# The second attention of a four-stage block: exponentials in f16 halves, turned by DMAs, on another timetable

## The chip, the cores and the metric

The kernel runs on one core of a Trainium2 chip. The metric is the device time of one launch in microseconds (us), the median of the timed runs. Engines are TensorE (PE, whose weight loads are PEld), VectorE (DVE), ScalarE (ACT), GpSimd (POOL) and SyncE (SP), which here issues DMAs.

## The reference

The input has 4096 tokens (2 sequences of 2048) of width 512, and for each sequence a context of 154 keys. Four stages add to `x` one after another: a masked attention, a mixture of 64 experts, a second attention without a mask, and a fused expert branch. The change is in the third:

```
x = x + tanh(g_xattn[1]) * attention(layernorm(x), ctx, ctx, wq, wk, wv)
Q = split(q @ wq.T);  K = split(k @ wk.T);  V = split(v @ wv.T)      # 16 heads of 32
attn = softmax(einsum('bhqd,bhkd->bhqk', Q, K) / sqrt(32))           # 2048 x 154 for each head
out = einsum('bhqk,bhkd->bhqd', attn, V)
```

Products that need f32 accuracy are either done in f32, or in f16 as three products of halves (`TERMS`: high by high, high by low, low by high), where a value is held as an f16 number and an f16 rest.

## The kernel before

`second_attention` (L913) works on 8 blocks of 512 tokens. A block has 4 tiles of 128 tokens and 16 heads in two groups of 8, so 8 *units* of one tile by 8 heads, and 64 units in the stage. Per unit:

- TensorE computes the 8 score matrices, 128 x 154 (L1064). They lie in two PSUM halves of 4 heads.
- VectorE takes the maxima of the first half out of PSUM (L1193), copies the second half to `sc` (L1195) and takes its maxima there (L1198).
- ScalarE computes exp(score - maximum) in f32 with the row sums (L1127), writing into `prob`, in which the 8 heads are interleaved. VectorE inverts the sums (L1181).
- The exponentials are needed with the keys on the partitions. TensorE turns them in ten 128 x 128 f32 transposes (L1013, `keys_turned`): one for the first 128 keys of each of 8 heads, and two for the 26 remaining keys of 4 heads together. ScalarE copies one of the three PSUM banks to `pT` (L1137), VectorE the other two (L1210).

Per block, TensorE further projects the queries (L55 with `wq`, 48 f16 matmuls), multiplies the turned exponentials by the values in f32, four groups of 4 heads (L1038 for the first 128 keys, L1040 for the rest, `V` and `VR`), and turns the result back (L1047). ScalarE copies the group's result (L1109), VectorE scales (L1171), GpSimd adds it to `x` (L1222). The rows of the coming blocks are normalised meanwhile: statistics (L126, L132), the normalised row (L148, VectorE), its f16 high half (L157, ScalarE), its low half (L166, VectorE here), and four DMA transposes (L175, SyncE). SyncE also loads a block (L62) and stores one (L1254), 1 MiB each.

Order: `plan` is one list of pieces per step of one unit, shared by all engines (`TURNS`, `VALS`, `FIN`); each engine walks through it in order. `NP = 3` buffers of exponentials, `NS = 2` of score halves. The stage ends with an all-engine barrier. Ahead of it TensorE already does two products of the next stage (`maps_ahead.tensor_first`), whose maps are loaded by `sync_ahead` after the store of block 6.

`first_attention` (L364) does nearly the same work in another form, and its rows are used below: exponentials in f32 (L650), rounded to f16 high halves by ScalarE in even units (L660, L661) and VectorE in odd ones (L774, L775), low halves by GpSimd (L807, L808), one DMA transpose for each half of a unit (L883), values in f16 with three terms (L568, L571), `NP = 2` buffers of halves and a timetable (`WHEN`) with a due time for each piece and engine. It has a mask, biases and an output projection besides.

## Time and profile before

| | |
|---|---|
| timed runs, median (lowest to highest) | 2776.18 us (2774.99 to 2778.49), 3 runs |
| profiled execution | 2766.97 us |
| its span, first to last instruction | 2765.2 us |
| TensorE busy | 2583.6 us (93%) |
| VectorE busy | 1599.7 us (58%) |
| ScalarE busy | 1390.0 us (50%) |
| GpSimd busy | 1121.0 us (41%) |
| mean granted TensorE clock | 0.983 of full speed |
| second attention, from its first maxima to the end of the stage | 1608.7 to 1944.7 us |

The shares over the whole span hide the stages: what bounds the second attention is read from stretches inside it. Busy time is the union of the instructions of an engine; in tables of groups, the means of neighbouring instructions overlap by some tens of ns.

### The profile page before, as it was taken

To read this page: it belongs to the slowest core of one execution; us is meant where nothing else is said; L and a number is where in the kernel's file an instruction comes from. 1 tells how busy PE (TensorE), PEld (TensorE's weight loads), DVE (VectorE), ACT (ScalarE), POOL (GpSimd) and SP (SyncE) were. 2 spreads that over 40 slices of the span, in tenths; PEclk is the share of its full clock that TensorE was granted. 3 is DMA by queue.
4 is the path that set the end of the run, shared out by engine and by line. 5 is a ranking of instruction groups with operands and counts; after the bars stand their busy time and mean duration, and the time that the engine had idled before them with its cause. 6 is when DMAs were issued, how large, how long until landed. Compare 5 with 4: busy or idle time off the path is not lost. (4 is left out here: it accounts for less than half of the span.)

```text
span 2765.2 us, 44090 instructions
## 1 busy us (share of the span) xinstructions
PE 2583.6 (93%) x16830; PEld 1404.4 (51%) x16830; DVE 1599.7 (58%) x2553; ACT 1390.0 (50%) x3074; POOL 1121.0 (41%) x887
## 2 busy tenths in 40 slices
PE   5788878999999999999999979998999999999999
PEld 3333333444444477777777645565444444444444
DVE  6799995655555365656556478887643332334232
ACT  4678884322322166666666468998433222222221
POOL 3577781565555656666666401011102211121111
PEclk8899999999999999999999989999999999999999
DMA  7799987222221299999999731322310111011000
GB/s 190 145 178 203 181 170 219 70 69 63 62 62 47 94 325 284 288 288 283 279 288 273 178 96 58 92 62 86 125 39 16 46 46 35 12 46 46 23 8 31
DMA packets 455409, 353.08 MB, mean 128 GB/s; under 512 B 323104, under 2 KB 332064, under 8 KB 455200
## 3 DMA queue, kind: packets, MB, share of 16 engines
q1 hardware_dynamic: 418336, 282.92, 36.6%
q0 software_dynamic: 36864, 67.34, 11.6%
q8 instruction: 135, 2.21, 0.3%
q14 instruction: 74, 0.61, 0.1%
HBM read 198.86 MB, written 75.89 MB: 99 GB/s over the span
## 5 line engine op out<-in xcount | busy, mean ns | idle before, releaser
L1673 POOL DMA_INDIRECT ids<-sh_tk,sh_su x256 | 267.8, 1046 | 231.0 <-PE sh_gu L55 75.0
L55 PE MATMUL ex_gu<-ex_xT,ex_h 128*128 128x256 f16 x3072 | 345.8, 273 | 2.3 <-ACT ex_xT L1946 1.7
L55 PEld LDWEIGHTS ex_gu<-ex_xT,ex_h 128*128 128x128 f16 x3072 | 300.1, 98 | 51.3 <-ACT ex_xT L1946 2.0
L2620 POOL TENSOR_TENSOR fe_prodT<-fe_pp,fe_prodT 128x512 f16<-128x512 f32 x64 | 77.4, 1210 | 591.3 <-ACT fe_prodT L2405 591.3
L2072 POOL DMA_INDIRECT xp<-ex_oo,ex_to x128 | 236.2, 1845 | 182.6 <-ACT ex_oo L1980 138.7
L1807 DVE SCALAR_TENSOR_TENSOR ex_h<-ring,ex_h 128x1024 f16<-128x1024 f32 x128 | 151.1, 1222 | 155.2 <-ACT ex_h L1797 155.2
L55 PE MATMUL at_g<-hm_zT,hm_w 128*128 128x512 f16 x768 | 184.7, 395 | 23.7 <-issue 16.1
L2536 DVE SCALAR_TENSOR_TENSOR ring<-fe_g,fe_nf,ring 128x512 f32<-128x512 f32 x32 | 24.0, 751 | 293.1 <-PE fe_g L2321 293.1
L55 PE MATMUL ex_o<-ex_h,ex_aT 128*128 128x512 f16 x768 | 181.2, 387 | 0.0
L1781 POOL DMA_INDIRECT ex_xg<-zrows,ex_idxu x128 | 158.3, 1237 | 49.2 <-issue 33.2
L650 ACT ACTIVATE at_s<-at_s,at_mx 128x154 f32<-128x154 f32 x512 | 168.5, 410 | 16.7 <-DVE at_mx L764 16.7
L55 PE MATMUL fe_g<-fe_up,fe_prodT 128*128 128x512 f16 x768 | 171.2, 380 | 3.2 <-DVE ring L2536 2.8
L1497 ACT ACTIVATE sh_si<-sh_gu 128x512 f32<-128x512 f32 x64 | 38.1, 596 | 264.0 <-PE sh_gu L55 263.9
L55 PE MATMUL sh_g<-sh_wdn,sh_actT 128*128 128x512 f16 x768 | 168.4, 379 | 1.1 <-DVE ring L1637 1.1
L1222 POOL TENSOR_TENSOR ring<-ring,at_sv 128x512 f32<-128x512 f32 x32 | 40.3, 1275 | 302.1 <-DVE at_sv L1171 302.1
L807 POOL TENSOR_TENSOR at_p<-at_s,at_p 128x1024 f16<-128x1024 f32 x64 | 132.3, 2067 | 57.1 <-DVE at_p L775 41.8
L55 PEld LDWEIGHTS at_g<-hm_zT,hm_w 128*128 128x128 f16 x768 | 74.9, 101 | 118.2 <-issue 41.8
L1616 DVE SCALAR_TENSOR_TENSOR sh_a<-sh_gu,sh_si 128x512 f32<-128x512 f32 x64 | 44.2, 691 | 152.1 <-ACT sh_si L1497 152.1
L2523 DVE TENSOR_TENSOR fe_t<-fe_p,fe_c 128x512 f32<-128x512 f32 x64 | 44.2, 691 | 150.0 <-ACT fe_c L2399 150.0
L1797 ACT ACTIVATE ex_h<-ring 128x1024 f16<-128x1024 f32 x128 | 128.0, 1053 | 2.4 <-DMA ring<-L_ffn_expert_gate_up_w 2.4
L55 PEld LDWEIGHTS fe_g<-fe_up,fe_prodT 128*128 128x128 f16 x768 | 73.3, 98 | 97.2 <-issue 5.9
L55 PEld LDWEIGHTS sh_g<-sh_wdn,sh_actT 128*128 128x128 f16 x768 | 74.1, 98 | 88.4 <-DVE ring L1637 1.2
(361 smaller groups left out, 5560.4 us busy)
## 6 DMA issues: line engine op xcount, KB each, us to landing
ring<-L_ffn_expert_gate_up_w SPq DMA_DIRECT2D x64, 1024.0 KB, 8.0
ring<-L_ffn_expert_down_w SPq DMA_DIRECT2D x64, 512.0 KB, 9.1
ring<-x SPq DMA_DIRECT2D x24, 1024.0 KB, 6.5
x<-ring SPq DMA_DIRECT2D x16, 1024.0 KB, 5.0
zrows<-hm_zs SPq DMA_DIRECT2D x32, 256.0 KB, 2.3
xp<-ring SPq DMA_DIRECT2D x8, 1024.0 KB, 5.3
out<-ring SPq DMA_DIRECT2D x8, 1024.0 KB, 4.3
ring<-xp SPq DMA_DIRECT2D x7, 1024.0 KB, 5.7
```

The source lines that it names most:

```text
L55: mm = nc.tensor.matmul(out, lhs(a, k), rhs(b, k), start=start and i == 0 and j == 0, stop=stop and i == n - 1 and j == 2)
L650: x = e.activation(to, to, ACT.Exp, bias=mx[i % 3][:, k:k + 1])
L807: e.tensor_tensor(first_keys(rows[:, 1, :]), sc[i % NS][:, :, 0:P], first_keys(rows[:, 0, :]), ALU.subtract)
L1222: e.tensor_tensor(x[:, k, :], x[:, k, :], scaled[n % 2][:, :], ALU.add).then_inc(s["x_out"], 1)
L1616: e.scalar_tensor_tensor(act32[k % 2][:, :], gu[k % 2][:, 1, :], 1.0 / WS, silu[k % 2][:, :], ALU.mult, ALU.mult).then_inc(s["a"], 1)
L1673: e.indirect_dma_start(ids, bass.IndirectOffsetOnAxis(slotu[b % 2][:, t, j:j + 1], 0), pair[b % 2][:, t, j, :], None, bounds_check=SLOTS - ...
L1781: self.nc.gpsimd.indirect_dma_start(self.xg[n % self.NG][:, :, :, :].rearrange("p h k n -> p (h k n)"), None, zrows, bass.IndirectOffsetOn ...
L1797: a.activation(w1[:, 0, k:k + 2, :], self.st1[x % 3][:, k:k + 2, :], ACT.Copy, scale=WS).then_inc(s["w1_hi"], 1)
L1807: v.scalar_tensor_tensor(w1[:, 1, k:k + 2, :], self.st1[x % 3][:, k:k + 2, :], WS, w1[:, 0, k:k + 2, :], ALU.mult, ALU.subtract).then_inc( ...
L2072: e.indirect_dma_start(dst, bass.IndirectOffsetOnAxis(to[:, n:n + 1], 0), o32[y % 2][:, t, :], None, bounds_check=T + SLOTS - 1, oob_is_er ...
L2523: e.tensor_tensor(t32[q % 2][:, :], trio[q % 2][:, 0, :], c32[q % 2][:, :], ALU.mult).then_inc(s["t"], 1)
L2620: e.tensor_tensor(prodT[:, 1, j, :], p32[q % 2][:, :], prodT[:, 0, j, :], ALU.subtract).then_inc(s["p_lo"], 1)
```

## The change

The second attention takes the form of the first. The exponentials are written in place into `sc` in f32, packed by head (`NS = 3`, now 8 heads wide). VectorE casts them to f16 high halves (`high`), GpSimd subtracts to get the low halves (`rest`), into `prob` (`NP = 2`, two halves each). SyncE turns each half of each unit by one DMA transpose of 128 x 1280 into `pT` (`turn_keys`). TensorE no longer turns keys, and neither ScalarE nor VectorE copies them out of PSUM. `V` and `VR` are f16 halves, and the product with the values has three terms. The low halves of the normalised rows move from VectorE to GpSimd. `plan` is replaced by a timetable per engine (`WHEN`, with `SECOND` and `THIRD` for blocks 1 and 2), in which each piece has a due time in units, and the two key turns of a unit stand next to each other (2.17 and 2.21). The maps of the next stage are asked for in four places.

```diff
             self.mine = sb("mine", [P, HG])
             self.KTn = [sb(f"KT{g}", [P, KT, CTX]) for g in range(BATCH)]
-            self.V, self.VR = [sb(f"V{g}", [P, D]) for g in range(BATCH)], [sb(f"VR{g}", [P, KT, P]) for g in range(BATCH)]
+            half = lambda n, s_: ctx.enter_context(nc.sbuf_tensor(f"at{layer}_{n}", s_, F16))
+            self.V = [half(f"V{g}", [P, 2, D]) for g in range(BATCH)]
+            self.VR = [half(f"VR{g}", [P, 2, KT, P]) for g in range(BATCH)]
...
-                                  self.mine[:, None, :, None].broadcast_to([P, KT, HG, HD]), ALU.mult)
+            rows, mine = (heads(bank.rearrange("p (g m) -> p g m", g=KT)),
+                          self.mine[:, None, :, None].broadcast_to([P, KT, HG, HD]))
+            high, low = (heads(self.VR[g][:, h, :, :]) for h in range(2))
+            v.tensor_tensor(high, rows, mine, ALU.mult).then_inc(s["v_hi"], 1)
+            v.wait_ge(s["v_hi"], 3 * g + 2)
+            v.tensor_tensor(low, rows, high, ALU.subtract).then_inc(s["v_hi"], 1)
+            v.wait_ge(s["v_hi"], 3 * g + 3)
+            out = v.tensor_tensor(low, low, mine, ALU.mult)
         else:
-            out = v.tensor_copy(self.V[g][:, :], bank)
+            v.tensor_copy(self.V[g][:, 0, :], bank).then_inc(s["v_hi"], 1)
+            v.wait_ge(s["v_hi"], 3 * g + 1)
+            out = v.tensor_tensor(self.V[g][:, 1, :], bank, self.V[g][:, 0, :], ALU.subtract)
         out.then_inc(s["v_out"], 1)
...
     UPB = 2 * TPB
     UNITS = NB * UPB
-    STEPS = UNITS + UPB
     NX = 5
-    NS = 2
-    NP = 3
-    behind = 1
+    NS = 3
+    NP = 2
...
-        sc = [sb(f"s{i}", [P, HG, CTX], F32) for i in range(NS)]
-
-
-        prob = [sb(f"p{i}", [P, HH * (P + HD)], F32) for i in range(NP)]
-        pT = [sb(f"pT{i}", [P, HH + 2, BLK], F32) for i in range(2)]
+        sc = [sb(f"s{i}", [P, HH, CTX], F32) for i in range(NS)]
+        prob = [sb(f"p{i}", [P, 2, HH * (P + HD)], F16) for i in range(NP)]
+        pT = [sb(f"pT{i}", [P, 2, HH + 2, BLK], F16) for i in range(2)]
...
+        WHEN = dict(
+            tensor=dict(project=(-4.34, -3.23, -2.22, -0.58), values=(8.45, 9.68, 10.08, 11.57),
+                        finish=(12.91, 14.28, 14.43, 16.53)),
+            scalar=dict(deviate=(-15.20,), prepare=(-12.81, -11.26, -10.91, -8.02), project=(-3.35, -2.89, -0.23, 1.70),
+                        values=(8.00, 10.14, 11.12, 11.26)),
+            vector=dict(stats=(-16.83, -16.21), prepare=(-13.10, -12.66, -12.35, -10.88),
+                        finish=(12.55, 14.05, 16.84, 18.76)),
+            gpsimd=dict(low=(-11.76, -10.85, -9.57, -6.62), finish=(14.08, 15.99, 18.24, 20.10)),
+            sync=dict(load=(-18.89,), turn=(-8.81, -8.53, -7.71, -6.44), store=(19.50,)))
+        SECOND = dict(
+            tensor=dict(), scalar=dict(deviate=(0.9,), prepare=(1.50, 1.55, 2.50, 2.55)),
+            vector=dict(stats=(0.3, 0.35), prepare=(1.20, 1.25, 2.20, 2.25)),
+            gpsimd=dict(low=(2.00, 2.03, 3.00, 3.03)), sync=dict(load=(-2,), turn=(2.65, 2.66, 3.40, 3.41)))
+        THIRD = {("scalar", "deviate"): 3.0, ("scalar", "prepare"): 4.5, ("vector", "stats"): 2.3,
+                 ("vector", "prepare"): 4.2, ("gpsimd", "low"): 5.0}
...
+        for i in range(UNITS):
+            at("tensor", i, "scores", i)
+            at("vector", i, "maxima", i)
+            for part, when in enumerate((0.81, 0.92)):
+                at("scalar", i + when, "exps", i, part)
+            at("vector", i + 1.25, "high", i)
+            at("vector", i + 1.29, "sums", i)
+            at("gpsimd", i + 2.51, "rest", i)
+            for part, when in enumerate((2.17, 2.21)):
+                at("sync", i + when, "turn_keys", i, part)
...
+        for i, m in enumerate((-9.5, -4.5, 1.0, 5.3)):
+            at("sync", UNITS + m, "maps_ahead", 0, i)
+
+        def pieces_of(engine):
+
+            return [piece[1:] for piece in sorted(due[engine], key=lambda piece: piece[0])]
...
+        def taken(i):
+
+            return s[f"keys{i % NP}"], 32 * (i // NP + 1)
+
+        def reused(e, i):
+
+            if i // TPB >= 2:
+                e.wait_ge(s["o_mm"], 2 * (i // TPB) - 2)
...
+            def values(B, u, gi):
+
+                n = 4 * B + 2 * u + gi
+                last = UPB * B + TPB * u + TPB - 1
+                g = B // NBB
+                e.wait_ge(s["v_out"], 2 * g + 2)
+                for parity in range(NP):
+                    e.wait_ge(*taken(last - (last - parity) % NP))
+                out = bank(("o", n), (s["o_hi"], n + 1))
+                ptb = pT[(2 * B + u) % 2]
+                grp = 2 * u + gi
+                heads = [(slice(j * HD, (j + 1) * HD), place(gi * HG + j)) for j in range(HG)]
+                for hv, hp in TERMS:
+                    for rows, k in heads:
+                        o = grp * P + rows.start
+                        e.matmul(out[rows, :], V[g][:, hv, o:o + HD], ptb[:, hp, k, :], start=(hv, hp) == TERMS[0], stop=False)
+                for hv, hp in TERMS:
+                    mm = e.matmul(out[:, :], VR[g][:, hv, grp, :], ptb[:, hp, HH + gi, :], start=False,
+                                  stop=(hv, hp) == TERMS[-1])
+                mm.then_inc(s["o_mm"], 1)
...
+            def exps(i, part):
+
+                e.wait_ge(s["neg"], 2 * i + part + 1)
+                if part == 0 and i >= NS:
+                    e.wait_ge(s["p_lo"], i - NS + 1)
+                if i >= 3:
+                    e.wait_ge(s["rsum"], i - 2)
+                for h in range(HG):
+                    k = HG * part + h
+                    to = sc[i % NS][:, k, :]
+                    x = e.activation(to, to if part else Sh[0][:, h, 0:CTX], ACT.Exp, bias=mx[i % 3][:, k:k + 1],
+                                     accum_out=sm[i % 3][:, k:k + 1])
+                x.then_inc(s["expd"], 1)
...
+            def maxima(i):
+
+                e.wait_ge(s["s_mm"], i + 1)
+                if i >= 3:
+                    e.wait_ge(s["expd"], 2 * (i - 2))
+                e.tensor_reduce(mx[i % 3][:, 0:HG], Sh[0][:, :, 0:CTX], AX.X, ALU.max, negate=True).then_inc(s["neg"], 1)
+                if i >= NS:
+                    e.wait_ge(s["p_lo"], i - NS + 1)
+                e.tensor_copy(sc[i % NS][:, HG:HH, :], Sh[1][:, :, 0:CTX]).then_inc(s["clip"], 1)
+                e.wait_ge(s["clip"], i + 1)
+                e.tensor_reduce(mx[i % 3][:, HG:HH], sc[i % NS][:, HG:HH, :], AX.X, ALU.max, negate=True
+                                ).then_inc(s["neg"], 1)
+
+            def high(i):
+
+                e.wait_ge(s["expd"], 2 * i + 2)
+                if i >= NP:
+                    e.wait_ge(*taken(i - NP))
+                if i < NP:
+                    e.wait_ge(s["blank"], NP)
+                e.tensor_copy(first_keys(prob[i % NP][:, 0, :]), sc[i % NS][:, :, 0:P])
+                e.tensor_copy(last_keys(prob[i % NP][:, 0, :]), rest_of(i)).then_inc(s["p_hi"], 1)
+
+            def sums(i):
+
+                e.wait_ge(s["expd"], 2 * i + 2)
+                to = inv[i // UPB % 3][:, i % TPB, i // TPB % 2 * HH:i // TPB % 2 * HH + HH]
+                e.reciprocal(to.rearrange("p (g j) -> p j g", j=HG), sm[i % 3][:, :].rearrange("p (j g) -> p j g", j=HG)
+                             ).then_inc(s["rsum"], 1)
...
+            def rest(i):
+
+                rows = prob[i % NP]
+                e.wait_ge(s["p_hi"], i + 1)
+                e.tensor_tensor(first_keys(rows[:, 1, :]), sc[i % NS][:, :, 0:P], first_keys(rows[:, 0, :]), ALU.subtract)
+                e.tensor_tensor(last_keys(rows[:, 1, :]), rest_of(i), last_keys(rows[:, 0, :]), ALU.subtract
+                                ).then_inc(s["p_lo"], 1)
...
+                elif what == "low":
+                    nrm.low(e, TPB * B + k)
...
+            def turn_keys(i, low):
+
+                if not low and i % TPB == 0:
+                    reused(e, i)
+                e.wait_ge(s["p_lo" if low else "p_hi"], i + 1)
+                e.dma_start_transpose(pT[i // TPB % 2][:, low, :, i % TPB * P:(i % TPB + 1) * P], prob[i % NP][:, low, :]
+                                      ).then_inc(s[f"keys{i % NP}"], 16)
...
+                elif what == "maps_ahead":
+                    maps_ahead.sync_ahead(A, k)
...
-    def sync_ahead(self, before):
-
-        for n in range(3):
-            self.nc.sync.wait_ge(*before.stored(3 + n))
+    def sync_ahead(self, before, n):
+
+        self.nc.sync.wait_ge(*before.stored(3 + n))
+        if n < 3:
             self.sync_map(n)
-        self.nc.sync.wait_ge(*before.stored(6))
-        sync_rows(self.nc, self.x[0], self.src, 0, self.s["x_in0"])
+        else:
+            sync_rows(self.nc, self.x[0], self.src, 0, self.s["x_in0"])
...
-    out["ctxR0"], out["ctxR1"] = rem.reshape(BATCH, D, P), rem.transpose(0, 1, 3, 2).reshape(BATCH, D, P)
+    out["ctxR"] = rem.reshape(BATCH, D, P)
```

## Rows read from the trace of the kernel before

**Rows 1.** stretches: length; PE, PEld, DVE, ACT, POOL busy (x); PEclk; DMA share; GB/s

```profile
1700.00:1860.00 160.00, 151.01 (x1251) 94.45 (x1250) 141.92 (x268) 147.57 (x605) 20.17 (x16) 1.00 0.27 69
150.00:350.00 200.00, 170.07 (x1412) 72.40 (x1412) 186.85 (x241) 163.65 (x413) 154.76 (x123) 0.97 0.95 189
1924.00:1945.00 21.00, 17.52 (x89) 7.91 (x88) 9.59 (x15) 8.59 (x29) 4.94 (x4) 0.92 0.63 220
```

**Rows 2.** L1193, whole trace and first block: ns min/median/max, first and last start

```profile
L1193 DVE TENSOR_REDUCE at_mx<-fe_g x64: 785/796/801, 1608.7 to 1923.7; 128x4 f32<-128x616 f32 x64
L1193 DVE TENSOR_REDUCE at_mx<-fe_g x8: 785/796/800, 1608.7 to 1651.5; 128x4 f32<-128x616 f32 x8
```

**Rows 3.** the waits, 1700 to 1860 us: us in total, times, longest

```profile
DVE at_pT L1210 <- PE at_g L1013: 16.0, 15, 2.1
ACT at_pT L1137 <- PE at_g L1013: 10.4, 14, 1.0
```

**Rows 4.** groups, 1700 to 1860 us: busy us, mean ns, idle before

```profile
L1013 PE MATMUL at_g<-id,at_p 128*128 128x128 f32 x320 | 52.3, 288 | 3.8 <-ACT at_p L1127 3.8
L1040 PE MATMUL at_g<-at_pT,at_VR 128*128 128x512 f32 x32 | 18.0, 645 | 0.0
L1038 PE MATMUL at_g<-at_pT,at_V 128*32 128x512 f32 x128 | 17.1, 605 | 0.0
L1137 ACT COPY at_pT<-at_g 128x512 f32<-128x512 f32 x33 | 19.3, 583 | 10.4 <-PE at_g L1013 10.4
L1210 DVE COPY at_pT<-at_g 128x512 f32<-128x512 f32 x32 | 22.0, 687 | 16.2 <-PE at_g L1013 16.0
L1210 DVE COPY at_pT<-at_g 128x256 f32<-128x256 f32 x32 | 13.2, 414 | 0.5
L166 DVE TENSOR_TENSOR hm_zs<-hm_z,hm_zs 128x512 f16<-128x512 f32 x16 | 10.9, 682 | 0.0
L148 DVE TENSOR_SCALAR hm_z<-ring,at_mv,at_rstd 128x512 f32<-128x512 f32 x16 | 8.0, 541 | 0.0
```

**Rows 5.** the same groups of the first attention, 150 to 350 us

```profile
L568 PE MATMUL at_g<-at_pT,at_V 128*32 128x512 f16 x216 | 15.0, 382 | 4.2 <-DVE ring L747 2.5 <-DMA at_pT<-at_p 1.8
L571 PE MATMUL at_g<-at_pT,at_VR 128*128 128x512 f16 x54 | 14.8, 383 | 0.0
L774 DVE CAST at_p<-at_s 128x1024 f16<-128x1024 f32 x17 | 15.4, 907 | 1.5 <-ACT at_s L650 1.2 <-DMA at_pT<-at_p 0.3
L775 DVE CAST at_p<-at_s 128x208 f16<-128x208 f32 x17 | 6.3, 373 | 0.0
L148 DVE TENSOR_SCALAR hm_z<-ring,at_mv,at_rstd 128x512 f32<-128x512 f32 x17 | 23.1, 1360 | 8.8 <-POOL hm_zs L166 8.8
L807 POOL TENSOR_TENSOR at_p<-at_s,at_p 128x1024 f16<-128x1024 f32 x35 | 72.1, 2060 | 21.5 <-DVE at_p L775 19.6 <-ACT at_p L661 1.9
L808 POOL TENSOR_TENSOR at_p<-at_s,at_p 128x208 f16<-128x208 f32 x35 | 22.7, 648 | 0.0
L166 POOL TENSOR_TENSOR hm_zs<-hm_z,hm_zs 128x512 f16<-128x512 f32 x18 | 21.8, 1212 | 8.4 <-ACT hm_zs L157 8.4
```

**Rows 6.** key turns back to back, then a plain transfer, by stretches

```profile
171.00:175.00 4.00, 3.86 (x57) 1.63 (x53) 3.97 (x5) 3.55 (x8) 4.00 (x4) 1.00 1.12 215
1740.00:1741.50 1.50, 1.50 (x8) 0.68 (x7) 1.50 (x4) 1.49 (x7) 0.00 (x0) 1.00 1.03 380
```

**Rows 7.** the waits of the first attention, 150 to 350 us

```profile
ACT at_p L660 <- DMA at_pT<-at_p: 8.8, 10, 2.6
```

**Rows 8.** tile at_p, 150 to 350 us: ns min/median/max; landing of its turns

```profile
L774 DVE CAST at_p<-at_s x17: 681/685/1728, 153.7 to 337.4; 128x1024 f16<-128x1024 f32 x17
DMA to landing us min/median/max: 3.4/3.7/8.0
```

**Rows 9.** timeline of the end of the stage

```profile
1931.11 1.36 PE L1038 MATMUL at_g<-at_pT,at_V 128*32 128x512 f32 x8 [1.08 <-DVE at_pT L1210]
1939.36 5.34 PE L55 MATMUL fe_g<-fe_h,hm_a 128*128 128x512 f16 x24
```

More of the change, by code:

```diff
@@ L967, in second_attention @@
-        for i, m in enumerate((1, 2)):
-            at(UNITS + m, "maps", 0, i)
-        rank = dict(low=0, turn=2, prepare=3)
-        for n in range(STEPS):
-            plan[n].sort(key=lambda what: rank.get(what[0], 1))
-        bank_of = {}
-        by_scalar = 1
-        def left(i, part):
-            if part < by_scalar:
-                return s["p_act"], by_scalar * i + part + 1
-            return s["p_vec"], (3 - by_scalar) * i + part - by_scalar + 1
-        def keys_of(pb, j):
-            if j < HH:
-                return pb[:, :].rearrange("p (n k) -> p k n", k=HH)[:, j, 0:P]
-            return pb[:, :].rearrange("p (n j) -> p j n", j=HH // HG)[:, j - HH, HG * P:]
@@ new lines, in at @@
+        def at(engine, when, what, b, k=0):
+            due[engine].append((when, what, b, k))
+        for engine, first in (("tensor", (-2, -1, 0.35, 1.35)), ("scalar", (-2, -1, 1.0, 1.9))):
+            for m, when in enumerate(first):
+                at(engine, when, "project", 0, m)
+        for i in range(UNITS):
[8 more added lines that the diff above has]
+                at("sync", i + when, "turn_keys", i, part)
@@ new lines, in second_attention @@
+        NORM = ("load", "stats", "deviate", "prepare", "low", "turn")
+        for b in range(NB):
+            for engine, pieces in WHEN.items():
+                for what, when in pieces.items():
+                    if b == 0 and what in NORM or b == 0 and engine in ("tensor", "scalar") and what == "project":
+                        continue
+                    if b == 1 and what in SECOND[engine]:
+                        when = [m - UPB for m in SECOND[engine][what]]
+                    if b == 2 and (engine, what) in THIRD:
+                        when = [max(m, THIRD[engine, what] - b * UPB) for m in when]
+                    for k, m in enumerate(when):
+                        at(engine, UPB * b + m, what, b, k)
@@ L1018, in piece @@
+            def piece(what, B, k):
+                if what == "scores":
+                    scores(B)
+                elif what == "values":
+                    values(B, *divmod(k, 2))
+                elif what == "project":
                     if k == 0:
```

238 lines of the change are left out of this document (57 added, 181 removed).

## The prediction

> **What bounds the kernel now.** I read the stretches first. The second attention works through 64 units (one tile of 128 tokens by 8 heads). Unit 0 starts at 1608.7 us, unit 7 at 1651.5 and unit 63 at 1923.7 [rows 2]. So the first seven intervals take 6.11 us each and the other 56 take (1923.7 - 1651.5) / 56 = 4.86 us. The even stretch from 1700 to 1860 us holds 160 / 4.86 = 32.9 units. Per unit TensorE is busy 151.0 / 32.9 = 4.59 us, ScalarE 147.6 / 32.9 = 4.49, VectorE 141.9 / 32.9 = 4.31 and GpSimd 20.2 / 32.9 = 0.61 [rows 1]. TensorE is the fullest, and the step is 4.86 / 4.59 = 1.06 of its work. The waits say the same: VectorE and ScalarE stand idle, 16.0 and 10.4 us in these 160, until TensorE has turned the keys (L1013) that they copy out [rows 3]. The DMA share is 0.27 [rows 1].
>
> The first attention already has the form that the change gives the second. It takes 200 us for 35 units, 5.71 each, with VectorE at 186.9 / 35 = 5.34, which is 1.07 below the step, and a DMA share of 0.95 [rows 1]. Its rows price what is new.
>
> **The change part by part, per unit.**
> *TensorE.* The ten turns of L1013 go: 52.3 / 32.9 = 1.59 us. The f32 products of values go, (18.0 + 17.1) / 32.9 = 1.07 [rows 4]. In f16 three terms take their place: 48 matmuls at 15.0 / 216 and 12 at 14.8 / 54 per block of 8 units, (3.33 + 3.29) / 8 = 0.83 [rows 5]. That leaves 4.59 - 1.59 - 1.07 + 0.83 = 2.76 us: TensorE stops being the bound.
> *ScalarE.* Its copy of turned keys goes, 19.3 / 32.9 = 0.59 [rows 4], which leaves 3.90. The exponentials stay, sums included; they now write packed f32 rows, not every eighth element. I count that at nothing, since their source is the same; if it is worth anything it is a gain on an engine that isn't late.
> *VectorE.* Two copies go, (22.0 + 13.2) / 32.9 = 1.07, and the low halves of the normalised rows move to GpSimd, 10.9 / 32.9 = 0.33 [rows 4]. That leaves 2.91. Added are the two casts to f16 for every unit. The first attention shows 0.91 + 0.37 = 1.28 in the mean [rows 5] and 0.69 + 0.37 = 1.06 with the large cast's median [rows 8]. L148 took 0.54 us here [rows 4] and 1.36 in the first attention beside a busy GpSimd [rows 5]; half of one per unit, that is 0 to 0.41 more. So VectorE needs between 3.97 and 4.60. I take 4.35, the mean cast with a third to a half of the L148 excess.
> *GpSimd.* The low halves of the exponentials are (72.1 + 22.7) / 35 = 2.71, the low halves of the rows 1.21 / 2 = 0.61 [rows 5], what it does today 0.61 [rows 1]: 3.93.
> *DMA.* Each unit sends two turns of 128 x 1280 f16, 327.7 KB. Back to back such turns moved 215 GB/s at a share of 1.12 [rows 6], so 1.52 us each and 3.05 for two. The four turns of rows per block, 262 KB each, at the same pace: 1.22 / 2 = 0.61. Load and store of a block, 1.05 MB each at 380 GB/s [rows 6], 2.76 x 2 / 8 = 0.69. Together 4.35. Packing them without gaps and with a faster pace for the rows' turns can't go below some 4.2. From above: the first attention's share is 0.95 x 5.71 = 5.42, and divided by the 1.12 that full pace shows, 4.84; it has masks to load besides [rows 1, 6].
> *Queues.* On SyncE 16 key turns per block now stand among the rows' turns, the load and the store. Each pair waits for the casts and then for GpSimd, and whatever stands behind it waits too; the load, issued a block ahead, can afford that, the rows' turns have some units. The maps for the next stage are asked for in four places and no longer in one; the split at the end used the first of them without a wait that mattered, so I count nothing. The longer preparation of V and VR lies in the stage before, under TensorE: nothing.
>
> So no engine is above 4.35, and two things stand there, VectorE and DMA. With the surcharge of 1.06 that both attentions show, the step is 4.35 x 1.06 = 4.61 us, say 4.62: 56 x (4.62 - 4.86) = -13.4 us. In the first seven intervals the two engines that must also prepare blocks 1 and 2 lose little work; bounds 0 and -5, I take -2.
>
> *The end.* Today the last values start at 1931.1 us and TensorE leaves the stage at 1944.7, partly at half clock (0.92 over the stretch) [rows 1, 9]. The last exponentials end at about 1929, which is the value product's start less the copy and the six turns. Then come casts 0.94, GpSimd 2.71, landing 3.7 [rows 5, 8]: values start some 7.6 us behind the exponentials, not 2.1, so 5.5 later. The values are shorter: two groups at 1.65 us, against two at (18.0 + 17.1) / 16 = 2.19 [rows 4, 5], so 1.1 less. Bounds +1 and +8 (the upper with these products at half clock too), I take +4.
>
> Sum: -13.4 - 2 + 4 = -11.4 us on the profiled execution's 2767.0 (its span is 2765.2), 2755.6. The median of the timed runs is 2776.2, 9.2 above it, so the forecast is **2765 us**.
>
> The Trainium skill ("Advanced Engine Details and Errata", section "X-Bar Transpose (TRN2)") says that turning DMAs are as fast as ordinary ones. Here the trace disagrees: 215 GB/s against 380 [rows 6]. By the rule DMA would need 1.05 MB / 380 GB/s = 2.8 us per unit, and VectorE alone would set the step; the sum would be the same, the second rival below would be smaller.
>
> **The rivals.**
> *Loose coupling (faster).* VectorE and DMA stay below ScalarE and GpSimd: casts at their median, no blocked L148, turns packed. Then the step is 3.93 x 1.06 = 4.17: -38.6 - 2 + 4 = -36.6, 2740 us. For it: GpSimd waits for the casts and not the reverse in most rows of the first attention. Against it: the DMA floor of 4.2.
> *The two buffers of halves bind (slower).* Casts of unit i+2 must wait until the low half of unit i has landed. That loop is casts 1.28, GpSimd 2.71, landing 3.7 and some 0.3 of handing over (an estimate): 8.0 us for two units, 4.0 each, if nothing lies in the way [rows 5, 8]. Per unit there are 1.2 us of other GpSimd work and 1.3 of other DMA work; if both always lie in the way, it is 10.5, or 5.25 each. The first attention, whose step leaves 11.4 for the loop, still had ScalarE idle 8.8 us on it [rows 7], and landings of up to 8.0 [rows 8]. At four fifths the step is 5.02: +9 - 2 + 4 = +11, **2787 us**; all of it, 2800. It makes the kernel slower once the mean loop passes about 9.7 us, two thirds in the way.
> *Blocked VectorE (slower).* The large cast took 1728 ns at worst against 681 at best [rows 8], and L148 2.5 times its time here [rows 4, 5], where GpSimd is busy 77% of the time [rows 1]. In the new stage it would be 85%. At 4.65 of VectorE the step is 4.93: +4 - 2 + 4 = +6, 2782 us.
> The Trainium skill ("SBUF — State Buffer", section "Who interferes with whom") has this as a lock: a copy, cast or scalar operation in its fast mode and a GpSimd instruction exclude each other for a whole instruction. The trace of the first attention agrees, with L148 at 1.36 against 0.54 us.
> *The clock.* TensorE would be busy 60% of the step, in bursts. Granted clock was 0.92 where it was busy 83% [rows 1]. At half clock everywhere it needs 5.5 us and is the bound again: +36 us and more. That all stretches fall is unlikely.
>
> **How the numbers follow.** The likeliest case 0.42, with its own range 2755 to 2772 (steps of 4.45 to 4.75); loose coupling 0.20; the two buffers 0.26; blocked VectorE 0.08; clock and others 0.04. What a measurement can't tell from no change is 0.2%, 5.5 us: 2770.6 to 2781.7. Faster: all of the loose case and nine tenths of the likeliest, 0.57. Same: the likeliest's rest, half of the blocked case, a third of the buffers near their turning point, 0.15. Slower: the rest, 0.28. The range 2736 to 2794 leaves out the half of the buffers' case beyond it, the clock and the best of the loose one.
>
> **What would show it.** Right: L1013 and both copies of L1137 and L1210 gone; starts of the first maxima 4.5 to 4.75 us apart; TensorE's busy share near 60%; DMA share above 1.0 in the stage; VectorE waiting for nothing long. Wrong: VectorE idle before its casts until a turn landed (the two buffers), casts and L148 well above 0.69 and 0.54 us (blocking), landings of the low half far above 3.7 us (DMA the bound), or a granted clock under 0.9 from 1660 to 1920 us. The stage's end more than 8 us later behind the last scores would break the end's term.

## The result

The changed kernel takes 2808.28 us (median of four runs, 2806.57 to 2809.62) against 2775.59 us for the kernel before in the same comparison (2774.50 to 2778.49). The ratio is 1.0115, 95% interval 1.0103 to 1.0127. It is 32.7 us slower where I forecast 11 us faster, and outside my range. (One execution of one kernel below, e4, took 7195 us, and its median leaves it out.)

The same stretch as in [rows 1], from 1700 to 1860 us, in the same columns (length; PE, PEld, DVE, ACT, POOL busy; PEclk; DMA share; GB/s), and the start of every first maxima, as in [rows 2], for the whole trace and for the first block:

```profile
1700.00:1860.00 160.00, 117.82 (x978) 57.77 (x976) 144.37 (x251) 125.10 (x552) 120.07 (x94) 0.81 1.06 202
```

```profile
L1158 DVE TENSOR_REDUCE at_mx<-fe_g x64: 741/792/802, 1622.3 to 1956.0; 128x4 f32<-128x616 f32 x64
...
L1158 DVE TENSOR_REDUCE at_mx<-fe_g x8: 765/799/800, 1622.3 to 1671.9; 128x4 f32<-128x616 f32 x8
```

The step is (1956.0 - 1671.9) / 56 = 5.07 us, where it was 4.86. Yet no engine is as full as TensorE was. TensorE went from 151.0 us of these 160 to 117.8 and ScalarE from 147.6 to 125.1. VectorE went from 141.9 to 144.4 and GpSimd from 20.2 to 120.1, and both have time left. The DMA share of 1.06 is near the 1.12 of [rows 6]; e7 below tests that. A stage that is slower while no engine is full is held by its waits. Here are those of the same stretch (engine, line, what it waited for: us in total, times, longest). In the changed kernel L1052 is the scores, L1119 the exponentials, L1173 and L1174 are the large and the small cast, L1219 is GpSimd's subtraction, L1071 and L1073 are the value products, L1141 is ScalarE's copy of their result, and L1250 the key turns:

```profile
PEld fe_g L1052 <- issue: 40.8, 31, 3.5
POOL at_p L1219 <- DVE at_p L1174: 38.8, 31, 2.4
PE fe_g L1052 <- ACT at_s L1119: 27.4, 17, 3.3
...
ACT at_oF L1141 <- PE at_g L1073: 16.2, 8, 2.5
PE at_g L1071 <- DMA at_pT<-at_p: 14.6, 4, 4.0
...
DVE at_p L1173 <- DMA at_pT<-at_p: 8.5, 12, 1.2
```

Two of them end at a key turn, and both are new. L1071 is the product of the turned keys with the values: TensorE stood still four times for up to 4.0 us until a turn had landed. L1173 is the large cast on VectorE: it waited 12 times until the turn that reads its buffer had landed. The large first rows are no sign of a loss by themselves: in e12, the fastest kernel below, the same three rows are 44.6, 28.4 and 32.0 us.

Where the 27.5 us of the stage stand, from the starts of the first maxima (unit 0, unit 7, unit 63) and the issue of the last store:

| profiled executions | units 0 to 7 | units 7 to 63 | unit 63 to last store | stage |
|---|---|---|---|---|
| before | 42.9 us | 272.2 | 20.3 | 335.4 |
| after | 49.7 | 284.0 | 29.2 | 362.9 |
| difference | +6.8 | +11.8 | +8.9 | +27.5 |

What follows the last store takes 821.2 and 821.1 us. What comes ahead of the stage differs by 13.6 us between these two executions (first maxima at 1608.7 and 1622.3), but that isn't shown to be the change's: two of the kernels below, e9 and e12, have the changed kernel's work ahead of the stage and start it at 1609.2 and at 1620.7. I therefore compare the lengths of the stage first, which are far steadier, and timed ratios second. The timed difference of 32.7 leaves 5 us beside the stage's 27.5 that I can't place.

The 56 even intervals aren't even. By the unit's place in its block of eight (its *slot*), the mean interval from its first maxima to those of the next unit:

| slot | 0 | 1 | 2 | 3 | 4 | 5 | 6 | 7 |
|---|---|---|---|---|---|---|---|---|
| before | 4.56 us | 4.74 | 4.71 | 4.95 | 5.52 | 5.04 | 4.66 | 4.69 |
| after | 4.64 | 4.32 | 6.90 | 5.49 | 3.80 | 5.38 | 4.16 | 5.89 |

Slot 2 loses 2.2 us in the mean, 1.5 to 3.6 in six of the seven blocks that it is counted in. Slot 7 loses 1.2, and slot 4 gains 1.7. The timeline of one such place (unit 42 to 43, maxima 7.5 us apart) shows why. First TensorE, then SyncE's issues (start us, us, what, with the idle time before it in brackets; for an issue the us are SyncE's own):

```profile
1849.36 0.46 PE L1052 MATMUL fe_g<-at_KT,at_qT 32*128 32x154 f32 x2
...
1853.53 1.47 PE L1071 MATMUL at_g<-at_pT,at_V 128*32 128x512 f16 x12 [3.70 <-DMA at_pT<-at_p]
1854.94 1.46 PE L1073 MATMUL at_g<-at_pT,at_VR 128*128 128x512 f16 x3
1856.33 0.63 PE L1052 MATMUL fe_g<-at_KT,at_qT 32*128 32x154 f32 x2
```

```profile
1845.47 1.59 SPq L175 DMA_TRANSPOSE hm_zT<-hm_zs  x1
1847.10 3.96 SPq L1250 DMA_TRANSPOSE at_pT<-at_p  x2
1851.12 1.43 SPq L175 DMA_TRANSPOSE hm_zT<-hm_zs  x1
```

At 1849.8 TensorE has finished scores. The next piece in its list is the third value product (due 10.08, slot 2), which needs the low half of unit 39. That half is in GpSimd until 1847.4, is asked for at about 1849.7 and lands at 1853.3. The 2.2 us between the first two are SyncE's queue: it issues without a pause here, so the high half, cast by 1844.8, is asked for only at 1847.1, behind a turn of rows, and the low half behind the high one. The next scores stand behind the product. They wait 3.7 us for it, then for its 2.8 us of work, and maxima, exponentials and casts wait with them.

The opening holds one such place, between the maxima of units 3 and 4, 12.7 us apart. A projection of block 1 stands ahead of scores there and waits for the rows' turns, the first of them issued 4.5 us before it:

```profile
1645.75 2.85 SPq L175 DMA_TRANSPOSE hm_zT<-hm_zs  x2
1648.65 2.91 SPq L1250 DMA_TRANSPOSE at_pT<-at_p  x2
```

```profile
1650.25 5.28 PE L55 MATMUL at_g<-hm_zT,hm_w 128*128 128x512 f16 x12 [6.55 <-issue]
```

And the end of the stage, against [rows 9]: the last values start 17.5 us after the last first maxima (1956.0) and not 7.4. The last pair of turns is issued behind a load of a map (L2149). First SyncE's issues, then TensorE:

```profile
1960.35 4.53 SPq L1250 DMA_TRANSPOSE at_pT<-at_p  x2
1964.92 0.69 SPq L2149 DMA_DIRECT2D ring<-L_ffn_W_K  x1
1965.66 5.62 SPq L1250 DMA_TRANSPOSE at_pT<-at_p  x2
...
1973.53 1.47 PE L1071 MATMUL at_g<-at_pT,at_V 128*32 128x512 f16 x12 [12.44 <-DMA at_pT<-at_p]
```

### The profile page after: what moved, and what is told of

Read it like the earlier page. It is cut to its first block and busy times, and to the rows that moved or that the text cites. A ratio compares the mean times of both kernels' runs of the same rounds, so it can differ in the third digit from the quotient of the medians.

```text
span 2806.3 us, 43235 instructions
## 1 busy us (share of the span) xinstructions
PE 2528.5 (90%) x16350; PEld 1334.7 (48%) x16350; DVE 1609.1 (57%) x2531; ACT 1354.7 (48%) x3010; POOL 1330.3 (47%) x1042
## 5 line engine op out<-in xcount | busy, mean ns | idle before, releaser
L1688 POOL DMA_INDIRECT ids<-sh_tk,sh_su x256 | 267.8, 1046 | 231.0 <-PE sh_gu L55 75.0
L55 PE MATMUL at_g<-hm_zT,hm_w 128*128 128x512 f16 x768 | 195.3, 411 | 31.3 <-DVE hm_b L693 11.6
L1219 POOL TENSOR_TENSOR at_p<-at_s,at_p 128x1024 f16<-128x1024 f32 x64 | 133.2, 2081 | 85.9 <-DVE at_p L1174 85.9
L817 POOL TENSOR_TENSOR at_p<-at_s,at_p 128x1024 f16<-128x1024 f32 x64 | 132.2, 2066 | 57.5 <-DVE at_p L785 42.7
L2538 DVE TENSOR_TENSOR fe_t<-fe_p,fe_c 128x512 f32<-128x512 f32 x64 | 44.3, 692 | 149.7 <-ACT fe_c L2414 149.7
L1995 ACT ACTIVATE ex_oo<-ex_o,ex_wt 128x512 f32<-128x512 f32 x128 | 81.2, 683 | 76.6 <-DMA xp<-ex_oo,ex_to 74.3
```

Source lines behind the costliest of these rows:

```text
L55: mm = nc.tensor.matmul(out, lhs(a, k), rhs(b, k), start=start and i == 0 and j == 0, stop=stop and i == n - 1 and j == 2)
L817: e.tensor_tensor(first_keys(rows[:, 1, :]), sc[i % NS][:, :, 0:P], first_keys(rows[:, 0, :]), ALU.subtract)
L1219: e.tensor_tensor(first_keys(rows[:, 1, :]), sc[i % NS][:, :, 0:P], first_keys(rows[:, 0, :]), ALU.subtract)
L1688: e.indirect_dma_start(ids, bass.IndirectOffsetOnAxis(slotu[b % 2][:, t, j:j + 1], 0), pair[b % 2][:, t, j, :], None, bounds_check=SLOTS - ...
L1995: e.activation(o32[x % 2][:, t, :], ob[t][:, :], ACT.Copy, scale=wt[:, n:n + 1]).then_inc(s["o_out"], 1)
L2538: e.tensor_tensor(t32[q % 2][:, :], trio[q % 2][:, 0, :], c32[q % 2][:, :], ALU.mult).then_inc(s["t"], 1)
```

## The experiments

All start from the changed kernel. "Stage" and the parts of it are measured as in the first table. The chips of the first eight runs were slower (before: 2796.2 and 2798.6 us there), so only ratios and stage lengths are compared with theirs. Each length comes from one profiled execution. e3 and e4, whose edits lie outside the steady part (units 7 to 63) but for two copies at its start, have 285.1 and 284.6 us there against 284.0; e1 and e11, alike in it but for the same two copies, differ by 2.6. So I call nothing under some 3 us of the steady part shown.

### e1: the third and fourth value products later

```diff
-            tensor=dict(..., values=(8.45, 9.68, 10.08, 11.57)
+            tensor=dict(..., values=(8.45, 9.68, 11.57, 11.60)
-                        values=(8.00, 10.14, 11.12, 11.26)),
+                        values=(8.00, 10.14, 12.00, 12.30)),
```

> Two of a block's four value products are due later (TensorE 11.57 and 11.60 for 10.08 and 11.57, ScalarE's copies 12.00 and 12.30). Theory V: the third value product stands in TensorE's queue ahead of the next unit's scores and waits there for the last key turn of its four units (23.6 us in 7 waits), which holds the scores: the interval between first maxima at slot 2 of a block falls from 6.9 to under 5.2 us, and the time from 2808 to about 2797 us. Rival B, the two buffers of halves set the pace: the wait reappears ahead of the casts, and the time stays at 2805 to 2810 us. Rival C, TensorE's half clock sets it: no change either, since TensorE gets no more work.

Measured: 2818.1 us, ratio 1.0074 (1.0048 to 1.0100). Units 7 to 63 take 278.0 us, 6.0 less. TensorE no longer waits in slot 2 (5.51 us), but both products now stand in slot 3, which goes from 5.49 to 6.39. So the wait was real, worth 6 of the 11.8 here. The casts' wait for turns stays, 21.5 us for 19.2.

### e2: three buffers of halves

```diff
-    NP = 2
+    NP = 3
```
(with a third semaphore, `keys2`)

> Three buffers of f16 halves for two; all else as changed. Theory B (two buffers): the casts no longer wait for landings (16.4 us in 17 waits today), the loop from cast to landing is spread over three units, steady step from 5.07 to 4.8 us or less, time 2790 us or less. Rival V (value products wait in TensorE's queue): the landings come hardly earlier, 2803 to 2809 us. Rival D (the DMA engines are at their limit): no gain, the waits move to the value products.

Measured: 2820.9 us, ratio 1.0075 (1.0052 to 1.0099). The cast never waits again, the last number being the idle time before it:

```profile
L1173 DVE CAST at_p<-at_s 128x1024 f16<-128x1024 f32 x64 | 53.2, 832 | 0.0
```

Yet units 7 to 63 take 281.5 us, 2.5 less, which is within the spread: slot 1 falls to 3.47 and slot 2 rises to 8.41. What is no longer held ahead of the value product is held at it. Alone, the two buffers are not the cause.

### e3: block 1's projections later

```diff
-            tensor=dict(), scalar=dict(deviate=(0.9,), ...
+            tensor=dict(project=(4.2, 5.2, 6.2, 7.2)), scalar=dict(project=(5.7, 6.7, 7.7, 8.3), deviate=(0.9,), ...
```

> Block 1's query projection is due at 4.2, 5.2, 6.2, 7.2 units for 3.66, 4.77, 5.78, 7.42, as the first attention has it; ScalarE's copies at 5.7, 6.7, 7.7, 8.3. Theory O: the 12.7 us between the first maxima of units 3 and 4 come from this projection, which waits for the turned rows with the scores of unit 4 behind it; time 2808 to about 2802 us, unit 3 to 4 under 8 us. Rival: those scores would wait for something else anyway (the exponentials, the rows), and the time stays within 2 us of 2808.

Measured: 2814.8 us, ratio 1.0059 (1.0041 to 1.0076). The first seven intervals take 40.6 us, 9.1 less than after and 2.3 less than before. The rest is unchanged (285.1 and 29.1 us). The projections' places, ahead of scores while their turns hadn't landed, were the whole loss of the opening.

### e4: the map load behind the last key turns

```diff
-        for i, m in enumerate((-9.5, -4.5, 1.0, 5.3)):
+        for i, m in enumerate((-9.5, -4.5, 1.3, 5.3)):
```

> The third map of the next stage is asked for at 65.3 units, behind the last key turns, for 65.0, ahead of unit 63's. Theory T: its 2.8 us of transfer lie ahead of the last key turn, which landed 6 us after its issue; the stage's end comes 2 to 3 us earlier, 2805 to 2806 us. Rival: the store and the load of x ahead of it hold it just as long, no change.

Measured: 2826.3 us, ratio 1.0086 (1.0062 to 1.0110). The end takes 27.5 us, 1.7 less; the rest is as after. SyncE's time for the load (0.69 us) was not what it cost, since the low half was asked for the moment GpSimd was done with it, in both kernels. What changed is the landing: the last low half lands 3.4 us after its issue (1988.4 to 1991.8) and not 6.0, when the map is asked for behind it. A small term.

### e5, e6: another timetable, with two and with three buffers

```diff
-    tensor: project=(-4.34, -3.23, -2.22, -0.58), values=(8.45, 9.68, 10.08, 11.57), finish=(12.91, 14.28, 14.43, 16.53)
+    tensor: project=(-3.6, -2.6, -1.6, -0.6), values=(8.45, 9.45, 11.2, 12.2), finish=(13.2, 14.2, 15.2, 16.2)
-    vector: finish=(12.55, 14.05, 16.84, 18.76)    gpsimd: finish=(14.08, 15.99, 18.24, 20.10)
+    vector: finish=(13.6, 14.6, 15.9, 16.9)        gpsimd: finish=(14.1, 15.1, 16.3, 17.4)
...
# ScalarE's copies and the rows' turns likewise; e3's and e4's edits too; e6 with NP = 3
```

> The changed kernel with another timetable and nothing else: value products of a block's second half at 11.2 and 12.2 units, their copies behind the exponentials of the unit and not ahead of them, query projections one per unit, the rows' turns not between the two halves of a key turn, block 1's projection later, the third map behind the last turns. From first maxima to last store the changed kernel takes 362.9 us, the kernel before 335.4. Theory V (pieces that wait in an engine's queue with scores or exponentials behind them): the stage falls to 335 to 342 us, step 4.65 to 4.75. Rival B (two buffers of halves) and rival D (DMA near its limit): the opening gains its 9 us, the step stays at 4.9 to 5.0 and the stage at 345 to 350 us.

> As e5, with three buffers of halves. Theory B+V (each hid the other): the waits ahead of the casts go, the step falls to 4.5 to 4.6 and the stage to 328 to 335 us. Rival D (DMA at its limit): no more than 2 us under e5. Rival V alone: within 3 us of e5.

Measured: e5 2837.5 us, ratio 1.0134 (1.0117 to 1.0151); e6 2814.0, ratio 1.0055 (1.0038 to 1.0072). Units 7 to 63 take 298.8 us in e5, a step of 5.34. My theory, that a table without waiting value products would suffice, failed. The waits of e5 between 1665 and 1925 us show one that I had put in myself:

```profile
POOL ring L1232 <- DVE at_sv L1203: 34.3, 15, 3.1
DVE at_p L1173 <- DMA at_pT<-at_p: 24.0, 20, 2.6
```

GpSimd's addition L1232 is due half a unit behind the division L1203 that it needs, but GpSimd's list runs about 1.25 units ahead of VectorE's by due times (`rest` of unit i is due at i + 2.51, its cast at i + 1.25). So it stands in front of the next `rest`, waits for VectorE, and the low halves, their turns and with two buffers the next casts are late. With three buffers the last link is cut: GpSimd's wait is still there (33.6 us, 18 times), but e6 takes 277.0 us, 21.8 less than e5. Its step is 4.95, not the 4.5 to 4.6 that I expected. The same third buffer that gave 2.5 us in e2 gives 21.8 here.

### e7: a fifth of the low turn

```diff
-    ... pT[...][:, low, :, ...], prob[i % NP][:, low, :]
+    nk = 2 if low else HH + 2
+    ... pT[...][:, low, 0:nk, ...], prob[i % NP][:, low, 0:nk * P]
```
e6, with 2 of the 10 blocks of each low half turned; the low halves of the other keys are left out of the products.

> As e6, but the DMA turns of the low halves carry 2 of their 10 blocks of 128 keys, so that most low halves of the exponentials are left out of the products (zeros stand there): 1.2 us less of DMA work per unit, all other instructions the same. Theory D (DMA sets the step or the landings): the stage is 10 us or more under e6. Rival E (the chain of scores, maxima and exponentials with VectorE sets it): within 4 us of e6.

Measured: 2805.1 us in one run; units 7 to 63 take 276.5 us against e6's 277.0. The two stretches from 1665 to 1925 us, e6 and then e7:

```profile
1665.00:1925.00 260.00, 192.43 (x1637) 93.94 (x1635) 240.99 (x397) 209.22 (x924) 200.79 (x150) 0.84 1.02 198
```

```profile
1665.00:1925.00 260.00, 191.09 (x1653) 93.47 (x1655) 243.03 (x398) 209.59 (x926) 200.53 (x150) 0.85 0.75 148
```

The DMA share falls from 1.02 to 0.75 and the step stays. With this table and three buffers the volume of the turns binds nothing. With two buffers a turn's landing is part of the loop from cast to cast, and no run shortened it there.

### e8: more work for TensorE

```diff
+            def more_work():
+                ...
+                for _ in range(5):
+                    e.matmul(gen[i][:, :], wq[:, 0, 0, 0:P], wq[:, 0, 1, :], start=True, stop=True)
```
called after each unit's scores; nothing reads the results.

> The changed kernel with 5 more f16 products of 128x512 behind each unit's scores, whose results nobody reads: 1.1 us of TensorE work per unit more. Theory K (half clock): the granted clock in the stage rises from 0.81 to 0.95 or more, projections and values take half as long where they were slow, and the stage gets shorter by 5 us or more in spite of the added work, under 358 us. Rival V or B: the clock rises but the stage stays at 360 to 368 us.

Measured: 2829.0 us in one run, stage 365.4. The stretch from 1665 to 1925 us:

```profile
1665.00:1925.00 260.00, 220.00 (x1767) 102.03 (x1768) 216.33 (x373) 193.59 (x855) 182.60 (x142) 0.93 0.99 190
```

The granted clock rose to 0.93 from 0.83 in the same stretch of after, and the stage grew by 2.5 us. Slot 2 is shorter (5.94 us for 6.90), slot 3 longer (6.23 for 5.49), and slots 5 and 7 are 5.11 and 5.66. The added products keep TensorE busy for 44.3 us between 1700 and 1860, 1.4 a unit, and this run can't tell their cost from what the faster products gave. What it shows is that both together return nothing. e9 shows that the loss can go without a higher clock.

### e9, e10: all four edits, and one piece to a gap

e9 is e1, e2, e3 and e4 together. e10 has three buffers, e4's edit and these due times:

```diff
+    tensor: project=(-2.6, -1.6, -0.6, 0.4), values=(9.2, 9.3, 11.2, 12.2), finish=(14.1, 14.2, 15.2, 16.2)
+    vector: stats=(-16.64, -14.64), prepare=(-13.70, -12.70, -11.70, -10.70), finish=(14.35, 15.35, 16.35, 17.35)
+    gpsimd: low=(-11.6, -10.6, -9.6, -8.6), finish=(15.6, 16.6, 17.6, 18.6)
+    sync: turn=(-6.60, -6.59, -5.60, -4.60), store=(19.90,)
...
# scalar to match; block 1: tensor project=(5.2, 6.2, 7.2, 8.4)
```

> The changed kernel with four edits at once: third and fourth value products and their copies later (as in e1), three buffers of halves (e2), block 1's projection later (e3), the map load behind the last key turns (e4). Stage means from the first maxima to the last store of the second attention: 335.4 us before, 362.9 after. Theory that each of these waits is a loss of its own and that two buffers bind once the products no longer wait: the opening takes 40.6 us for seven units (49.7 after), units 7 to 63 take 262 to 270 us (284.0), the end 27.5 (29.2): stage 330 to 338, at or a little under the kernel before. Rival, lumps: a unit's loop scores, maxima, exponentials, scores takes 3.7 us, and a unit is longer wherever more pieces stand in one gap of TensorE's or VectorE's list than fit into it; taking waits away leaves the gaps with two pieces (slots 3, 5 and 7 of eight at 5.3 to 6.4 us): units 7 to 63 take 273 to 278, stage 342 to 347.

> As e9, but every piece has another due time: one projection or one or two value products in a gap of TensorE's list (projections in slots 5, 6, 7 and 0, values in 1, 1, 3 and 4), one normalization or one division in a gap of VectorE's, GpSimd's additions 1.25 units behind the divisions they need. Theory lumps: no slot is above 5.2 us and the mean step is 4.5 to 4.7 us, since VectorE's own work is 4.36 us a unit: units 7 to 63 take 252 to 263 us, stage 322 to 332 with a tail of 29, under the 335.4 of the kernel before. Rival, waits only: with the waits gone alike in both, it takes what e9 takes, within 3 us. Rival, the load of VectorE and the memory: the step stays at 4.9 or more as in e6 (4.95), whatever the order.

Measured: e9 2776.5 us against 2773.9 for before, ratio 1.0010 (0.9997 to 1.0023); e10 2781.7, ratio 1.0026 (1.0017 to 1.0036). e9's parts are 41.0, 267.8 and 26.2 us, stage 335.1. The loss is gone: 27.8 us less in the stage than after, with the form of the work unchanged, one buffer more, and a granted clock of 0.84 from unit 7 to 63, where it was 0.81. The steady part falls by 16.2 us, where e1 and e2 alone gave 6.0 and 2.5. e9's first maxima and its large cast:

```profile
L1158 DVE TENSOR_REDUCE at_mx<-fe_g x64: 740/799/801, 1609.2 to 1918.1; 128x4 f32<-128x616 f32 x64
```

```profile
L1173 DVE CAST at_p<-at_s x64: 676/692/2014, 1616.9 to 1922.9; 128x1024 f16<-128x1024 f32 x64
its engine sat idle before it (us, times) until:
  DMA at_pT<-at_p: 0.6, 1
```

The rival, lumps, was half right: slot 3 with two value products, a projection and two normalizations is 7.19 us long. But e10, made to spread everything, has 6.32 in slot 3 and 5.56 in slot 1, and takes 271.5 us, 9 to 20 more than expected. ScalarE waits there for rows' turns (1665 to 1925 us):

```profile
ACT hm_zs L157 <- DMA hm_zT<-hm_zs: 16.5, 7, 4.4
POOL hm_zs L166 <- ACT hm_zs L157: 14.7, 10, 3.6
```

I had put the rows' turns so late that ScalarE's high halves, and GpSimd's low ones behind them, stood still until a buffer of rows had been turned.

### e11, e12: e9 with two buffers, and e9 with slot 3 thinned out

```diff
# e11: e9 with NP = 2
# e12: e9 and
-    tensor: project=(-4.34, -3.23, -2.22, -0.58)     scalar: project=(-3.35, -2.89, -0.23, 1.70)
+    tensor: project=(-3.90, -2.80, -1.70, -0.58)     scalar: project=(-3.05, -2.05, -1.05, 1.70)
-    vector: prepare=(-13.10, -12.66, -12.35, -10.88)
+    vector: prepare=(-13.10, -12.66, -11.66, -10.66)
```

> e9 with the two buffers of halves that the change has, so three of the four edits. Units 7 to 63: 284.0 us after, 267.8 in e9. Theory that the buffers bind once the products no longer wait: a cast again waits until the turns of two units ago have landed, a loop of about 9 us for two units, and units 7 to 63 take 275 to 280 us, the kernel 0.3 to 0.5% more than e9. Rival, that the third buffer is worth only what it gave alone (2.5 us): 268 to 271, the time within 0.15% of e9's.

> e9 with the gap that is now the longest thinned out: between the maxima of units 3 and 4 of eight (7.19 us) TensorE has two value products and a projection, VectorE two normalizations. The first projection goes one gap on, the second and third up to half a unit on, and two normalizations one gap on. Theory lumps: that gap falls to 5.2 to 6.0 us, the next ones rise by 0.5 together, the mean step goes from 4.78 to 4.65, units 7 to 63 take 258 to 263 us and the kernel 2765 to 2770 us, under the one before. Rival, VectorE's load: whatever leaves the gap comes back in the next ones, and units 7 to 63 stay within 2 us of 267.8.

Measured: e11 2784.0 us, ratio 1.0037 (1.0023 to 1.0051); e12 **2765.5 us** against 2775.5, ratio 0.9970 (0.9958 to 0.9983), faster than both kernels. e11 takes 280.6 us from unit 7 to 63, 12.8 more than e9, and its casts wait again:

```profile
L1173 DVE CAST at_p<-at_s x64: 678/694/1647, 1620.1 to 1940.2; 128x1024 f16<-128x1024 f32 x64
its engine sat idle before it (us, times) until:
  DMA at_pT<-at_p: 29.6, 20
```

So the two buffers bind once the value products don't. The due times alone, without the third buffer, take the stage to 348.5 us, 14.4 of the 27.8 that e9 gives. e12 takes 261.7 us there, a step of 4.67; slot 3 falls from 7.19 to 5.76 and slot 4 rises by 0.51 only. The rival, that VectorE's load brings it all back, fell: 6.1 us stayed gone. The stage is 330.3 us long, 5.1 less than before the change, and the timed difference is 10.0, so about half of that gain isn't placed in the stage. The stretch of [rows 1] in e12:

```profile
1700.00:1860.00 160.00, 118.62 (x1044) 57.60 (x1043) 150.82 (x263) 134.07 (x583) 130.64 (x99) 0.86 1.11 211
```

VectorE is at 150.8 of 160 us, 94%, the share that TensorE had before.

## Why the prediction was wrong

**Which step failed.** "With the surcharge of 1.06 that both attentions show, the step is 4.35 x 1.06". The surcharge is the step over the work of the fullest engine. I took it from two stages with other orders of work and assumed that waits would add as little whatever the new order was. In the new order they added more. Here are the 56 even intervals of the kernel before, of after and of e12, in the columns of [rows 1]:

```profile
1651.50:1923.70 272.20, 254.52 (x2137) 160.44 (x2138) 235.16 (x442) 249.02 (x1029) 35.33 (x28) 0.99 0.25 65
1671.90:1956.00 284.10, 204.38 (x1728) 101.17 (x1731) 243.94 (x423) 221.67 (x985) 204.12 (x159) 0.81 1.03 197
1661.90:1923.60 261.70, 194.57 (x1724) 95.07 (x1722) 245.34 (x423) 223.21 (x985) 209.07 (x159) 0.85 1.11 212
```

The surcharge was 272.2 / 254.5 = 1.07 over TensorE before. It is 284.1 / 243.9 = 1.16 over VectorE after, and 261.7 / 245.3 = 1.07 in e12. VectorE does the same work in after and in e12, within 0.6%, and the steps are 5.07 and 4.67. So it is the waits that differ.

**The loads were near, but for TensorE's.** The stretch from 1700 to 1860 us has 160 / 5.07 = 31.6 units by the mean step. Divided by that, ScalarE takes 3.96 us a unit (3.90 forecast), GpSimd 3.80 (3.93), VectorE 4.57 (4.35, bounds 3.97 to 4.60) and TensorE 3.73 (2.76; the rows that I priced it from were at a granted clock of 0.97 to 1.00, and this stretch is at 0.81). Over all 56 intervals, in whose last blocks no rows are left to prepare, VectorE takes 243.9 / 56 = 4.36. If 4.57 is put into my sum, the step is 4.84 and the steady part -1 us, not -13; by this reading half of the miss would be load. But e12 needs 4.40 in its stretch and 4.38 over all, as much as after, and has a step of 4.67. My 4.62 was there to be had, within 0.05 us, with other due times and one more buffer. What I didn't do was to read the table of due times piece by piece: which wait of a piece can be long, and what stands behind it.

**What the surcharge hid.** I priced SyncE's queue ("whatever stands behind it waits too") and never TensorE's. Scores of the next unit stand behind a value product (due 10.08) that needs a turn due 0.87 units before it (9.21), 4.4 us, while a landing alone takes 3.3 to 8.8 us; in the timeline above TensorE was ready for the product 0.1 us after the turn had been issued. In the trace of before this place had no such wait, since TensorE turned the keys itself. e1 shows 6.0 us of it; with three buffers it is 13.7 (e9 against e2, with e3's and e4's edits too).

Nor did I price SyncE's own time. Its issues between unit 7 and unit 63, added up from the trace, take 232.1 us of 284.1 in after, 4.14 a unit. In the mean a high half was asked for 1.27 us after its cast and a low half 0.98 us after GpSimd was done with it, up to 3.9. So part of every late landing is this queue, and no run changed that alone. It need not bind: e7 has 0.6 us a unit less of it than e6 and the same step, and in e12 the issues fill 251.4 us of 261.7 and the delays are 2.9 and 2.1 us. I had also written that the two turns of a unit stand next to each other; once a block a turn of rows (due -8.81, between the .17 and .21 of a pair) stands between them.

**The two buffers.** This rival had the step and, the clock aside, the time that came nearest (5.02 and 2787 us, against 5.07 and 2808). It had a loop of 8.0 us plus what lies in the way, 10 at four fifths; the loop from cast to landing is 8.9 us in the mean after and up to 13.6. A mean loop of 8.9 for two units would allow a step of 4.45, so that 5.02 came so near is partly luck: the buffers bind at single units, and they are one cause of two. The third buffer gives 2.5 us alone (e2, within the spread), 12.8 with the other three edits (e11 against e9) and 21.8 beside a worse table (e6 against e5). The two causes hide each other: single edits (e1, e2) summed to 8.5 us in the steady part, and together they gave 16.2. I read this as one loop through all engines, in which the wait that is left takes up what the other gives back.

**The opening**: -2 forecast, +6.8 measured. I argued from the work of the engines again. e3, with block 1's due times for the projections changed, gives -2.3 against before, which is what I forecast.

**The end**: +4 forecast (bounds 1 and 8), +8.9 measured. The last values start 17.5 us behind the last first maxima. Behind the last exponentials (they end at 1960.1) come 2.3 us until the large cast, and for 1.96 of these VectorE stands idle, until the turn of unit 61's low half has landed:

```profile
1962.40 0.69 DVE L1173 CAST at_p<-at_s 128x1024 f16<-128x1024 f32 x1 [1.96 <-DMA at_pT<-at_p]
```

It loses little by that, since GpSimd is busy with unit 62's low half until 1963.5 and starts on the last one at 1963.7, 3.6 us behind the exponentials where I had 0.9 for the casts. The low half then takes 3.6 us and not 2.7, and its turn 6.0 from issue to landing and not 3.7. Of the last two value products the first takes 1.47 and 1.46 us for its two parts, the second 0.96 and 0.82. e4 takes 1.7 off the end, e9 3.0.

**Not the cause.** The volume of the turns: the share falls to 0.75 from 1.02 and the step stays (e7, beside e6's table and three buffers). The Trainium skill ("Advanced Engine Details and Errata", section "X-Bar Transpose (TRN2)") holds that such a DMA is as fast as an ordinary one. The stretches that I read don't agree: 215 GB/s back to back against 380 [rows 6], and 211 at a share of 1.11 in e12. The rule would have done no harm, since the share didn't bind.

The clock: its sign came true (0.81 from unit 7 to 63, under my 0.9), and this rival's +36 us is nearest the measured 32.7. But it had TensorE as the bound at 5.5 us a unit, and TensorE takes 3.73. In e9 the loss is gone at 0.84, and e12 is faster than the kernel before at 0.85. What a full clock would add to either isn't shown.

Blocked VectorE: L148 has a median of 1534 ns between 1700 and 1860 us, against a mean of 541 in [rows 4], beside a GpSimd that is busy 75% of the time, and the large cast a mean of 852. This fits "SBUF — State Buffer", section "Who interferes with whom" of the Trainium skill, by which a cast or scalar operation in its fast mode and a GpSimd instruction hold each other up for a whole instruction. Which of the two is hit depends on the table: in e12, with GpSimd busy 82%, L148 is back at a median of 491, and the large cast has 834 where it had 693. VectorE's sum is the same in both, so this doesn't explain the loss. No run took the blocking away, so what it costs in all isn't shown.

**What stays open.** Slots 3, 5 and 7 are still long in e12 (5.76, 4.87 and 5.64 us). Slot 7 is above 5.6 in after and in every experiment but e10, where it is 5.19. In all tables but that one it holds both pieces of VectorE's statistics (due 7.17 and 7.79); e10 moves one of them, and much else. I didn't try to even the slots further, and don't know how much of the surcharge of 1.07 is left in them, nor whether VectorE or SyncE sets the step of e12.

## What to carry to other kernels

When work moves from an engine to a queue, list for each engine the pieces that stand in front of the critical loop's next piece, and for each what it waits for and when that is ready at the latest. Count the time of the engine that issues the DMAs too. A ratio of step to load taken from another order of work is no forecast of that. When a single edit returns less than its wait, keep it and cut the next wait before judging it: waits in a coupled loop hide each other. And where a stage gets slower while no engine is full, look at order and buffers before load: here other due times returned half of the loss (e11), and with one more buffer all of it (e9).

## What the runs showed of the hardware

- The mean granted clock from unit 7 to 63 was 0.81 in after, 0.84 in e9 and 0.85 in e12, with stages of 362.9, 335.1 and 330.3 us, so 27.8 to 32.6 us came back at nearly the same clock. With added products that nobody reads the clock was 0.93 (1665 to 1925 us) and the stage 365.4 (e8).
- One turn of 128 x 1280 f16 costs SyncE 1.25 us at least and 1.43 in the median to issue, and lands 3.3 to 8.8 us later, 3.7 in the median. The two turns of a unit take over half of SyncE's time in a step of 5.07 us, and a turn of rows in front takes 1.3 to 1.6 us more in the timelines above. Of the lines below, the first has ns at least, in the median and at most; the next two say who waited for a landing (us, times); the last is from issue to landing:

```profile
L1250 SPq DMA_TRANSPOSE at_pT<-at_p x128: 1252/1430/4209, 1630.9 to 1967.3; - x128
...
  PE at_g L1071: 36.1, 8
  DVE at_p L1173: 19.2, 19
...
DMA to landing us min/median/max: 3.3/3.7/8.8
```
